# The last round's terms from ScalarE and final additions on VectorE, x's sums first in a round, a short solve of step 1

## The reference

```python
x = x + conv_ref(gn(x), w, b, w_child, b_child, gate)   # 3x3, ternary weights
x = x + omp_ref(gn(x), dictionary)

# omp_ref, for B = 16*16*16 = 4096 patches, D: [512, 256]
G = D.T @ D + 1e-5 * eye(256);  h_bar = (D.T @ X).T;  h = h_bar
for k in range(1, 6):
    index = argmax(abs(h * ~mask), axis=1); mask[patch, index] = True
    # w from a triangular solve with G[I, index]; the corner is sqrt(clip(1 - sum(w*w), 1e-5))
    # x_stack from two triangular solves
    h = h_bar - x_stack @ G[I]
coeffs[I] = x_stack
recon = D @ coeffs, put back as patches
```

## Time and profile before

| | us |
|---|---|
| median of 3 runs | 535.72 |
| lowest, highest | 534.46, 536.69 |
| the profiled execution's own time | 535.57 |
| its span | 533.5 |
| busy: TensorE, VectorE, ScalarE, GpSimd | 414.8, 458.1, 307.7, 150.2 |
| mean granted clock of TensorE | 0.927 of full |

### The profile page before, as it was taken

How to read it: one execution, slowest core, us unless ns; L and a number is a source line. 1 busy time by engine, 2 the same in 40 slices (tenths; PEclk the granted TensorE clock), 3 DMA queues, 4 the chain that set the end, 5 groups by cost and what they waited for, 6 DMA issues and landing times.

```text
span 533.5 us, 7603 instructions
## 1 busy us (share of the span) xinstructions
PE 414.8 (78%) x1756; PEld 303.0 (57%) x1756; DVE 458.1 (86%) x2324; ACT 307.7 (58%) x680; POOL 150.2 (28%) x162
## 2 busy tenths in 40 slices
PE   0089974999792969999865699998929788978684
PEld 0033862556682945468754555577828566766453
DVE  4765668899999799989999799999997989999990
ACT  2535448866477188777665598686703444465133
POOL 3000034443300255444000745323004644330010
PEclk9999997999988879999996989999978979999598
DMA  5999912899200036999400564314002753234156
GB/s 99 176 142 149 143 40 71 142 175 156 50 2 0 29 90 135 191 172 162 90 1 2 130 146 105 94 41 108 12 0 58 168 125 99 65 79 88 31 108 130
DMA packets 110203, 50.72 MB, mean 95 GB/s; under 512 B 103632, under 2 KB 104144, under 8 KB 110160
## 3 DMA queue, kind: packets, MB, share of 16 engines
q1 hardware_dynamic: 101592, 26.13, 29.8%
q0 software_dynamic: 8160, 24.13, 19.4%
q10 hardware_dynamic: 408, 0.00, 0.0%
HBM read 34.24 MB, written 8.65 MB: 80 GB/s over the span
## 4 chain that ended last, share of the span: by engine, by line
PE 43%; DVE 38%; issue 6%; ACT 6%; SPq 3%; DMA 3%; POOL 0%; DVEq 0%; ACTq 0%
PE h L374 28%; PE conv_ps L374 12%; DVE junk L1020 10%; DVE coef L1141 5%; DVE top L950 4%; DVE top_i L963 4%; SPq L244 3%; DVE top_i L965 2%; ACT score L661 2%; DVE mask L1047 2%; DMA rows<-gram,idx_u 2%; ACT diag L670 1%; PE back_ps L374 1%; DVE coef L1137 1%; ACT xb L627 1%
## 5 line engine op out<-in xcount | busy, mean ns | idle before, releaser
L346 POOL DMA_INDIRECT rows<-gram,idx_u x128 | 131.8, 1030 | 326.8 <-DVEq L1007 297.6
L374 PE MATMUL h<-rows,diag 128*128 128x256 f32 x640 | 152.6, 394 | 29.0 <-ACT diag L670 28.0
L374 PEld LDWEIGHTS h<-rows,diag 128*128 128x128 f32 x640 | 123.3, 197 | 59.2 <-issue 39.7
L670 ACT ACTIVATE diag<-ident,dx 128x128 f32<-128x128 f32 x320 | 96.8, 387 | 45.6 <-DVEq L1122 42.0
L1020 DVE SCALAR_TENSOR_TENSOR junk<-mask,rows 128x256 bf16<-128x256 bf16 x320 | 119.1, 418 | 0.0
L661 ACT ACTIVATE score<-h 128x512 f32<-128x512 f32 x80 | 47.3, 598 | 89.9 <-PE h L374 89.1
L950 DVE MAX8 top<-score 128x8 f32<-128x256 f32 x160 | 65.0, 419 | 18.6 <-ACT score L661 17.1
L374 PE MATMUL back_ps<-coef_t,d_t 128*128 128x256 f32 x224 | 58.4, 419 | 15.0 <-ACT coef_t L676 15.0
L374 PE MATMUL h<-d_sb,z 128*128 128x256 f32 x256 | 67.6, 428 | 2.3 <-DVEq L941 2.3
L374 PEld LDWEIGHTS h<-d_sb,z 128*128 128x128 f32 x256 | 63.6, 329 | 6.3 <-DVEq L941 3.1
L374 PE MATMUL conv_ps<-xa,w_taps 128*64 128x512 f32 x128 | 62.6, 612 | 4.0 <-DVEq L1205 4.0
(11 more groups left out here) (149 smaller groups left out, 526.5 us busy)
## 6 DMA issues: line engine op xcount, KB each, us to landing
xa<-in_x SPq DMA_DIRECT2D x64, 128.0 KB, 4.4
out<-x SPq DMA_DIRECT2D x64, 128.0 KB, 2.9
x<-y POOLq DMA_DIRECT2D x14, 512.0 KB, 4.9
xb<-in_x SPq DMA_DIRECT2D x48, 128.0 KB, 4.8
rows<-gram,idx_u POOLq DMA_INDIRECT x128, 3.1
xb<-in_x SPq DMA_DIRECT2D x16, 120.0 KB, 5.3
d_sb<-in_L_conv_dictionary SPq DMA_DIRECT2D x4, 128.0 KB, 3.8
gram<-coef_t SPq DMA_DIRECT2D x1, 256.0 KB, 2.2
```

The source lines that it names most:

```text
L346: pool.indirect_dma_start(out=rows[s][:, k, t, :], out_offset=None, in_=gram_dram[:, :], in_offset=bass.IndirectOffsetOnAxis(ap=idx_u[s][: ...
L374: return nc.tensor.matmul(dst, lhs, rhs, start=start, stop=stop, skip_group_check=skip)
L670: last = nc.scalar.activation(diag[s][:, t, j, :], ident[:, :], ACT.Copy, scale=dx[s][:, k, t, j:j + 1])
```

## The change

- **Terms on ScalarE.** In the last round the last `ACT_TERMS` = 2, 2, 1, 1 coefficients of images m = 0 to 3 are no longer added by VectorE. ScalarE writes mask x coefficient as tiles of their own (`make_terms`, in the unused space of `z`), and TensorE sums them with VectorE's tile in PSUM by products with the identity (`sum_terms`), which transpose in the same pass.
- **Additions on VectorE.** `residual` is gone. For images 14 and 15 VectorE adds PSUM to the image in `x1`, half by half. The store of image 14 is issued by ScalarE, behind its last copy.
- **Order at the end.** The reconstruction of image 14 is split around `sum_terms` of image 15, and image 15 has a copy of its transposed coefficients of its own (`last_coef_t`).
- **x's sums.** In rounds 1 and 2 `x_sums` stands first in TensorE's round. `variance` stands where it stood.
- **Step 1's solve.** For k = 1 it has one pair of operations (the negated square and the negated entry) where it had five, then the same four as before. At step 4 the generator has one more wait, for `x_last`.

```diff
@@ last_images, TensorE
-                pe.wait_ge(h_read[0], STEPS * ROUNDS)
-                for half in (1, 0):
-                    residual(n + 2, half, end_ps[2][half])
                 for m in range(2):
-                    coef_transposes(r, m, final_ps)
+                    sum_terms(r, m)
                     for q, half in enumerate((1, 0)):
                         pe.wait_ge(y_done, 2 * (n + m) + q + 1)
-                        add_atoms(n + m, half, end_ps[m][half], True)
+                        add_atoms(n + m, half, end_ps[m][half])
+                sum_terms(r, 2)
+                pe.wait_ge(h_read[0], STEPS * ROUNDS)
+                add_atoms(n + 2, 1, end_ps[2][1])
+                sum_terms(r, 3)
+                add_atoms(n + 2, 0, end_ps[2][0])
                 pe.wait_ge(h_read[1], STEPS * ROUNDS)
                 for half in (1, 0):
-                    residual(n + 3, half, end_ps[3][half])
-                for m in range(2, IMG_R):
-                    coef_transposes(r, m, final_ps)
-                    for half in (1, 0):
-                        add_atoms(n + m, half, end_ps[m][half], False)
+                    add_atoms(n + 3, half, end_ps[3][half], last_coef_t)
+            def sum_terms(r, m):
+                n = IMG_R * r + m
+                pe.wait_ge(terms_ready, m + 1)
+                for i in range(ACT_TERMS[m] + 1):
+                    if i == ACT_TERMS[m]:
+                        pe.wait_ge(coef_ready, n + 1)
+                    for k in range(CHUNKS):
+                        for t in range(2):
+                            part = coef[:, m, t, :] if i == ACT_TERMS[m] else terms[m][:, i, t, :]
+                            last = mm(final_ps[:, k, t * P:(t + 1) * P], part[:, k * P:(k + 1) * P], ident[:, :],
+                                      i == 0 and k == 0 and t == 0, i == ACT_TERMS[m], True)
+                last.then_inc(coef_t_ps, 1)
@@ the end, ScalarE
+            make_terms(ROUNDS - 1, 0)
+            make_terms(ROUNDS - 1, 1)
+            copy_coef(ROUNDS - 1, 0, final_ps)
+            out_back(ROUNDS - 1, 0, end_ps[0])
+            copy_coef(ROUNDS - 1, 1, final_ps)
+            make_terms(ROUNDS - 1, 2)
+            make_terms(ROUNDS - 1, 3)
+            out_back(ROUNDS - 1, 1, end_ps[1])
+            copy_coef(ROUNDS - 1, 2, final_ps)
+            copy_coef(ROUNDS - 1, 3, final_ps, last_coef_t)
+            act.wait_ge(image_added[0], 2)
...
@@ the end, VectorE
-                for j in range(STEPS):
+                for j in range(STEPS - ACT_TERMS[m] if r == ROUNDS - 1 else STEPS):
...
+                    dve.wait_ge(recon_ps, 2 * n + q + 1)
+                    v.tensor_tensor(part, part, end_ps[m][half][:, :, :], ALU.add).then_inc(image_added[m - 2], 1)
@@ body, TensorE
+                if front and behind:
+                    x_sums(f)
                 if behind:
                     coef_transposes(b, 0)
                 correlate(r, 1)
-                if front:
+                if front and not behind:
                     x_sums(f)
@@ solve, VectorE
+                if k == 1:
+                    c = step(v.scalar_tensor_tensor(out=n_inv[s][:, :, 1, 0], in0=g_at[s][:, :, 0], scalar=-1.0,
+                                                    in1=g_at[s][:, :, 0], op0=ALU.mult, op1=ALU.mult))
+                    step(v.tensor_scalar(n_inv[s][:, :, 1, 1], g_at[s][:, :, 0], -1.0, None, ALU.mult))
+                    yield
+                else:
+                    yield from new_row(s, k, w)
...
-                    step(v.tensor_reduce(x_last[s][:, :, :], dx[s][:, :, :, :].rearrange("p k t j -> p t j k"), AX.X, ALU.add))
+                    c = step(v.tensor_reduce(x_last[s][:, :, :], dx[s][:, :, :, :].rearrange("p k t j -> p t j k"), AX.X, ALU.add))
+                    yield
+                    after(c)
+                    dve.sem_inc(x_last_ready[s], 1)
```

More of the change, by code:

```diff
@@ L136, in build_program @@
         iota_i = junk[:, 0:2, :].rearrange("p a n -> p (a n)").bitcast(U32)
+        spare_z = z[:, :, :].rearrange("p m n -> p (m n)")
+        terms = []
+        for m in range(IMG_R):
+            first = 2 * ATOMS * sum(ACT_TERMS[:m])
+            terms.append(spare_z[:, first:first + 2 * ATOMS * ACT_TERMS[m]].rearrange("p (i t n) -> p i t n", t=2, n=ATOMS))
+        first = 2 * ATOMS * sum(ACT_TERMS)
+        last_coef_t = spare_z[:, first:first + CHUNKS * 2 * P].rearrange("p (k n) -> p k n", k=CHUNKS)
         h = [ctx.enter_context(nc.psum_tensor(f"h{s}", [P, TILES, ATOMS], F32)) for s in range(2)]
@@ L199, in build_program @@
         coef_ready = sem("coef_ready")
+        x_last_ready = [sem(f"x_last_ready{s}") for s in range(2)]
+        terms_ready = sem("terms_ready")
+        image_added = [sem(f"image_added{m}") for m in range(2)]
         coef_t_ps = sem("coef_t_ps")
@@ L306, in _ @@
             body(ROUNDS - 1, False, False, True)
-            for m in range(IMG_R):
+            for m in (0, 1, 3):
                 store(ROUNDS - 1, m)
@@ L472, in coef_transposes, with add_atoms @@
                 last.then_inc(coef_t_ps, 1)
-            def residual(n, half, to):
-                for c2 in range(2):
-                    c = 2 * half + c2
-                    mm(to[:, c2, :], ident[:, :], x1[:, n % KEPT, c:PIX:PATCH], c2 == 0, False, True)
-            def add_atoms(n, half, to, first):
+            def add_atoms(n, half, to, rows_t=coef_t):
                 pe.wait_ge(coef_t_done, n + 1)
@@ L484, in add_atoms @@
                     for k in range(CHUNKS):
-                        last = mm(to[:, c2, :], d_t[:, k, 2 * half + c2, :], coef_t[:, k, :], first and c2 == 0 and k == 0,
+                        last = mm(to[:, c2, :], d_t[:, k, 2 * half + c2, :], rows_t[:, k, :], c2 == 0 and k == 0,
                                   k == CHUNKS - 1, True)
@@ L803, in _, with make_terms @@
             body(ROUNDS - 1, False, True)
-            for m in range(IMG_R):
-                copy_coef(ROUNDS - 1, m, final_ps)
-                out_back(ROUNDS - 1, m, end_ps[m])
+            def make_terms(r, m):
+                s = m // 2
+                act.wait_ge(x_last_ready[s], ROUNDS)
+                for i in range(ACT_TERMS[m]):
+                    j = STEPS - ACT_TERMS[m] + i
+                    for t in range(2):
+                        tile = 2 * (m % 2) + t
+                        last = nc.scalar.activation(terms[m][:, i, t, :], mask[s][:, j - 1, tile, :], ACT.Copy,
+                                                    scale=x_last[s][:, tile, j:j + 1])
+                last.then_inc(terms_ready, 1)
+            make_terms(ROUNDS - 1, 0)
[9 more added lines that the diff above has]
+            act.wait_ge(image_added[0], 2)
+            for q in range(PATCH):
+                act.dma_start(out[BY_DMA][:, q:H:PATCH, :],
+                              image_of(x1, BY_DMA)[q * C:(q + 1) * C].rearrange("p (g w) -> p g w", w=W)).then_inc(y_stored, 16)
         @block.vector
```

61 lines of the change are left out of this document (34 added, 27 removed).

## The result

| | before | changed |
|---|---|---|
| median of the runs on the same chip, us | 537.01 (9 runs, 534.46 to 539.57) | 533.56 (9 runs, 532.20 to 534.97) |
| ratio, 95% interval | | 0.9928 (0.9901 to 0.9955) |
| profiled execution, us | 535.57 | 534.21 |
| its span, us; outside the span | 533.5; 2.07 | 531.2; 3.01 |

The change makes the kernel 0.7% faster: 3.9 us of the 535.72 that I started from, where 4.2 were forecast. The two profiled executions are nearer to each other than that: 2.3 us of span, and 0.94 of it is taken back outside the span (3.01 against 2.07). So the forecast is not borne out by its sum, and it is read place by place. Outside the span the kernel before takes 1.98 to 2.10 in all 65 executions that ran beside the experiments.

The account below looks back on a forecast made before the run. TensorE bounds the middles of rounds 0 to 2, an alternating chain the last round, a serial chain the end. +0.2 + 0.4 - 1.4 - 3.4 = -4.2 from 535.57 gives 531.4 us; forecast 530.0 to 532.9, range 528.8 to 534.3.

Parts of the forecast that it names:

- the four terms: Sums at round starts +0.2, added x_last wait +0.4, step 1's solve -1.4, the end -3.4 us.
- What bounds the kernel: TensorE is full in the middles of rounds 0 to 2; the last round alternates between engines; the end is serial.
- The sums, +0.2: x's sums ahead of round 2's transposes cost 0.2 us, bounds 0 and 0.5; round 1 has room, gain 0.
- The added wait, +0.4: VectorE's wait for x_last at step 4, 0.15 us each; +0.4 over rounds 0 to 2, bounds 0 to +0.6.
- Step 1's solve, -1.4: Last round: diagonals 1.0 us earlier, about 0.4 from the other set's saved operations; bounds -0.5 and -1.9.
- Rival 1: Clock falls in the last round's step 2 after a wait of about 3 us; 534.3 us, chance 0.17.
- The end, -3.4: Last images finish 3.6 us earlier, less 0.2 for the clock; bounds -4.1 to -0.5.
- rival 2: TensorE's term passes at the end cost as much as 256-column ones; 534.3 us, chance 0.08.
- The addition: VectorE's last addition, PSUM plus x1 at a stride of four values: 0.9 us, between 0.6 and 1.1.
- The clock at the end: Low at 494.3 us, rising during the term passes at no cost or in image 12's atoms; +0.2 us taken.
- Rival 4: Low clock holds through the end; at the low clock throughout, 547 us; chance 0.03.
- The sum: All terms together -4.2 us against the profiled 535.57, so 531.4 us, 0.8% less.

Follow-up runs that it names:

- e1: Kernel before with the short solve of step 1 alone; 535.87 us, ratio 0.9979.
- e2: Kernel before with the new end alone: long solve, sums behind the transposes, added x_last wait in the last round only; 533.77 us, ratio 0.9974.
- e11: Changed kernel with x's sums back behind the transposes and the x_last wait in the last round only; 533.60 us, ratio 0.9920.
- e4: Changed kernel with VectorE's four last additions packed instead of at a stride of four values; 535.26 us, one execution.
- e6: Changed kernel with longer filling ahead of last-round step 1 and 2 updates, sums back behind transposes, x_last wait in last round only; 530.61 us, ratio 0.9888.
- e9: e5 with x's sums alone put back behind the transposes; 534.28 us, ratio 0.9934.
- e7: e6 with a third term of image 12 on ScalarE and 12 filling products ahead of the last images' transposes; 530.52 us, ratio 0.9885.
- e8: e7 without the filling products at the end; 530.54 us, ratio 0.9899.
- e10: e5 with the x_last wait alone put back to the last round only; 532.87 us, ratio 0.9921.
- e5: Changed kernel with more filling products on TensorE ahead of the last round's step 1 and step 2 updates; 533.15 us, ratio 0.9939.
- e12: e7 with 30 filling products ahead of the first transposes of rounds 1 to 3, 18 ahead of rounds 1 and 2's second add-back; 535.14 us, ratio 0.9955.

## Why the prediction came out as it did

The time came out near the forecast, but the terms did not: by the traces each of the four terms came out worse than I had put it down.

**What bounds the kernel** held: no saving in rounds 0 to 2 showed (T is 398.06 with e1's short solves, 397.90 before), and what the traces gain from T on is in the last round and the end.

**The sums, +0.2.** Round 2 costs 0.44, at the bad end of my bounds, since the transposes start 0.45 behind the two small passes at the low clock and the chain waits for all of it. Their gain of 0 and their free place in round 1 were right.

**The added wait, +0.4.** 0.24 to 0.26 a time where I took 0.15. Together the two cost 0.9 at the round starts, not 0.6; they overlap in round 1. That T moved by 0.73 does not confirm it, since T scatters by 1.5 to 2.1 between equal programs.

**Step 1's solve, -1.4.** This step failed, and in two ways. Its start was right: the diagonals are 0.92 earlier. Then I took VectorE's wait of 1.00 for a gain of the solve. That wait stood behind an update at the low clock, and it goes with a faster update and the long solve as well (e2). The solve's own worth up to step 2, at equal clock, is 0.63 and not 1.4. And the path behind it failed: I left TensorE's clock in step 2 as it was. Rival 1 came true as it was written: the wait ahead of step 2's update grew to 3.23 and the clock fell, which cost 1.69 here and 2.96 in e1. I gave it 0.17, though I had worked out the wait of about 3 myself and had a fall after 3.32 and none after 2.51. I argued against it with the fall in step 1, whose wait was to shrink to 2.3. It shrank to 2.65 and the clock still fell there, between 428.0 and 428.5, and was low until after 431. The wait's length alone does not decide it: in e11 step 1's wait was 2.41 and its update was slow too (5.37).

**The end, -3.4.** It brought 3.0. Taken back by U3's shift of 0.70, image 14's own tile starts at 513.22 where I had 512.85, mostly because VectorE waits 0.2 behind each of the two `x_last`, where I had 0.1 for both. From there to the last product TensorE takes 524.79 - 513.92 = 10.87 against 10.85 worked out: the term passes are 0.11 apart, (1.95 - 0.27) / 15, as the transposes of the same shape were, and rival 2 fell. The addition took 1.08, at the upper bound and not in the middle, as the strided ScalarE write of the earlier trace rows and the Trainium skill's rule on 16-byte lines had it (SBUF — State Buffer, Door 1); e4 shows that the stride is the cause. The clock at the end was free, as worked out: 0.54 or less from 494 to 500, 1.00 from there, and TensorE still waits 1.02 for VectorE at 513.92. Rival 4 did not happen; its 547 is also misadded, since products that end near 541 instead of 527 give 549.

**The sum.** By the cuts: +0.7 (rounds), -1.7 (up to U2; 0.63 is the solve's own worth, most of the rest the faster update at U1), +1.7 (the clock behind U2), -3.0 (end), or -2.3 of span where I had -4.2. The profiled execution took 534.21, which is rival 1's 534.3. The medians are 3.45 apart. What is between them no trace explains: before's median is 1.4 above its own profiled execution, and its longer executions (540.96 at a granted clock of 0.915 beside 535.28 at 0.921, in one series) were never the profiled one. So that the forecast of 531.4 lies 0.5 from 535.72 x 0.9928 = 531.9 is luck: the solve in it was worth nothing here. What I left out, the scatter between executions of each kernel, is as large as the terms that missed. A part of it is where the clock rises and falls; whether that is all is not shown.

**Best version.** e6 and its two relatives are the fastest kernels measured: 530.61, 530.52 and 530.54 against 536.06, 1.0 to 1.2% under before and, by their ratios, about 0.4% under the changed kernel, though the intervals still overlap (0.9901 to 0.9955 there, 0.9860 to 0.9917 in e6). In the traces e6 has the 0.9 at the round starts and the 1.7 of step 2's clock over the changed kernel. How much of the lead in the medians these make, and whether e9 to e11 (0.9920 to 0.9934) were merely unlucky, stays open.

## What to carry to other kernels

When a wait of one engine ends beside a slow update, ask first what made the update slow; the wait is then not sure to be the saved operation's gain. Where TensorE idles in a serial chain, a shorter step elsewhere lengthens its idle time, and the clock may take back the whole saving. Products to an unread bank in that idle time kept the clock up ahead of step 2's update in seven kernels of seven, and in three of them it fell one step later, so read the whole chain behind it. Size them in passes and from a measured duration (an fp32 product of 256 columns is two passes of 0.22 here), and shorter than the wait. An operation that is moved ahead of a chain costs its length there unless what waits for it is itself late: 0.44 in round 2, 0.05 in round 1. And compare two programs that are equal up to a point before a difference at that point is put down to an edit.

## What the runs showed of the hardware

- The same idle time costs differently. After 9.42 to 9.44 us of it the 32 products took 8.46 us in e6 and 9.96 in e11, programs that are equal up to there; after 2.36 us, 32 products took 7.14 (e6, e7, e8, e10) or 8.83 and 8.69 (e5, e9, e12). What decides it isn't shown.
- VectorE's 512-element addition with one operand in PSUM takes 0.69 packed and 1.08 at a stride of four values, a ratio of 1.57; ScalarE's copies of 512 elements out of PSUM take 0.60 packed and 1.10 at that stride.
- The kernel with the highest mean granted clock (e12, 0.983) was slower than the one at 0.945 (e7), 0.7% by the ratios: its filling outlasted the waits and made TensorE's next work 3.0 to 3.3 us late.
